# Sweeping groups of images: both halves' channel products first, then both halves' inverse y products

## What is computed

```python
def _fourier_layer(v, W1, W2):
    x_ft = jnp.fft.rfft2(v)
    out1 = jnp.einsum('bixy,ioxy->boxy', x_ft[:, :, :M1, :M2], W1)
    out2 = jnp.einsum('bixy,ioxy->boxy', x_ft[:, :, -M1:, :M2], W2)
    ...
    return jnp.fft.irfft2(out_ft, s=(Sx, Sy))
...
for i in range(L):
    x1 = _fourier_layer(v, W1, W2)
    x2 = jnp.einsum('bcxy,cd->bdxy', v, w_w[i]) + w_b[i][None, :, None, None]
    v = x1 + x2
    ... # normalised over images and pixels, then relu
```

## Time and profile before

| | |
|---|---|
| median of 3 runs | 2758.26 us (2756.05 to 2761.63) |
| profiled execution | 2755.14 us, its span 2753.4 us |
| TensorE busy | 2334.1 us, 85% of the span |
| VectorE busy | 1924.8 us, 70% |
| ScalarE busy | 1050.1 us, 38% |
| inverse y products, L794 | 24576 matmul records, 237 ns each on average |
| channel products, L1029 | 6144 matmul records in the three sweeps |
| mean DMA rate | 187 GB/s |

### The profile page before, as it was taken

How to read it: one execution, slowest core, us unless ns; L and a number is a source line. 1 busy time by engine, 2 the same in 40 slices (tenths; PEclk the granted TensorE clock), 3 DMA queues, 4 the chain that set the end, 5 groups by cost and what they waited for, 6 DMA issues and landing times. The chain is left out here.

```text
span 2753.4 us, 191399 instructions
## 1 busy us (share of the span) xinstructions
PE 2334.1 (85%) x88271; PEld 1444.0 (52%) x88271; DVE 1924.8 (70%) x3293; ACT 1050.1 (38%) x1799; POOL 500.5 (18%) x619
## 2 busy tenths in 40 slices
PE   5799999977999997789999975876499826899998
PEld 3466666644666665456666642222277712444444
DVE  5688888865888886668888854004588863677776
ACT  3433333352333332523333333002136623677776
POOL 1034422200444221024442200000223200000000
PEclk9899999997999999989999997898789958999999
DMA  3266666615999996179999964896234203788886
GB/s 86 57 152 168 170 163 163 170 40 186 322 322 320 313 314 185 58 253 325 328 315 310 311 215 159 314 415 118 81 93 113 66 14 82 125 141 143 144 141 100
DMA packets 243410, 515.84 MB, mean 187 GB/s; under 512 B 65423, under 2 KB 114895, under 8 KB 222223
## 3 DMA queue, kind: packets, MB, share of 16 engines
q1 hardware_dynamic: 233736, 504.07, 64.4%
q10 hardware_dynamic: 9495, 9.34, 1.6%
HBM read 295.39 MB, written 214.78 MB: 185 GB/s over the span
## 5 line engine op out<-in xcount | busy, mean ns | idle before, releaser
L923 ACT ACTIVATE p_v<-p_ps,k_scale_bias 128x1024 f32<-128x1024 f32 x384 | 441.8, 1200 | 883.8 <-PE p_ps L794 883.8
L904 POOL COPY k_xm<-p_sp 64x288 f32<-64x288 f32 x372 | 260.2, 700 | 1181.0 <-DVE p_sp L327 1164.8
L317 DVE STREAM_TRANSPOSE p_vt<-p_v 128x1024 f32<-128x1024 f32 x384 | 451.2, 1213 | 6.4 <-ACT p_v L923 6.4
L794 PEld LDWEIGHTS p_ps<-k_idfty,p_t 32*64 32x64 f32 x24576 | 292.0, 135 | 178.5 <-issue 178.4
L2201 DVE TENSOR_TENSOR x_ht<-x_ht,x_mask 128x384 f32<-128x384 f32 x512 | 262.0, 554 | 149.7 <-ACT x_ht L2172 102.2
L2172 ACT ACTIVATE x_ht<-x_ph,w_b 128x384 f32<-128x384 f32 x576 | 303.4, 578 | 142.4 <-PE x_ph L2224 142.4
L322 DVE STREAM_TRANSPOSE p_at<-p_ps 128x1024 f32<-128x1024 f32 x192 | 228.5, 1228 | 149.6 <-PE p_ps L295 149.6
L794 PE MATMUL p_ps<-k_idfty,p_t 32*64 32x64 f32 x24576 | 319.8, 237 | 10.7 <-issue 10.7
L803 PEld LDWEIGHTS p_ps<-p_vt 128*32 128x32 f32 x24576 | 219.6, 109 | 99.8 <-issue 99.8
L2224 PE MATMUL x_ph<-x_et,w_w 64*64 64x384 f32 x2304 | 247.0, 494 | 12.7 <-DMA x_et<-expert_inputs 6.4
L2240 PE MATMUL x_pe<-x_ht,w_w 64*64 64x384 f32 x2304 | 245.0, 489 | 11.3 <-DVE x_ht L2201 10.2
(11 more groups left out here) (329 smaller groups left out, 2625.4 us busy)
## 6 DMA issues: line engine op xcount, KB each, us to landing
field<-p_v SPq DMA_DIRECT2D x768, 256.0 KB, 5.8
p_v<-field SPq DMA_DIRECT2D x128, 1024.0 KB
x_mask<-expert_weights SPq DMA_DIRECT2D x32, 1536.0 KB, 14.8
l_v<-field SPq DMA_DIRECT2D x16, 2048.0 KB, 25.8
k_xm<-field SPq DMA_DIRECT2D x12, 2048.0 KB, 28.7
at_cf<-state_coefficients SPq DMA_DIRECT2D x32, 384.0 KB
k_mixw<-field SPq DMA_DIRECT2D x4, 2048.0 KB, 26.1
k_mixw<-in_L_tok_fw_dram SPq DMA_DIRECT2D x48, 144.0 KB, 4.4
```

Of the source, the lines that this page charges most:

```text
L317: return nc.vector.transpose(cols(vt), cols(px.rearrange("p (g m) -> p g m", g=G)))
L794: ins = nc.tensor.matmul(ps[64 * a1:64 * a1 + 64, g, col:col + S], lines, K["idfty"][rows, :], start=False, stop=True, skip_group_check=True)
L904: nc.gpsimd.tensor_copy(view[64 * k:64 * k + 64, :, j, :, G * i:G * i + G], sp[64 * j:64 * j + 64, :, :, 16 * k:16 * k + M1].rearrange("p ...
L923: nc.scalar.activation(field[:, 2 * q:2 * q + 2, CH * half:CH * half + CH], ps[:, e, 2 * q:2 * q + 2, :], ACT.Relu, bias=bias, scale=scale ...
```

## The change

In each group the channel products of both halves are issued first, and then the inverse y products of both halves. The wait of half 0 for its own inverse turn is dropped, since the wait of half 1 for both turns now stands ahead of both inverse y products. Prologue and loop are changed alike. The number of instructions other than that wait stays the same, and VectorE's, ScalarE's, GpSimd's and SP's orders aren't touched.

```diff
                         nc.tensor.matmul(ps[C * a:C * a + C, e, g, :], weights[rows, C * g:C * g + C], v[rows, 0, col:col + CH],
                                          start=True, stop=False, skip_group_check=True)
-                if half == 0:
-                    pe.wait_ge(s.t_ready, 2 * i + 1)
-                    pe.nop(nofuse=True)
-                inverse_y(nc, K, ps[:, e], st, half).then_inc(s.um_done, 1)
+
+            def rows(i):
+                for half in range(2):
+                    inverse_y(nc, K, ps[:, half], st, half).then_inc(s.um_done, 1)
...
             pixels(0, 0)
             pixels(0, 1)
+            rows(0)
             spectrum(1)
             with pe.Fori(1, n) as i:
                 pixels(i, 0)
                 pixels(i, 1)
+                rows(i)
                 forward(i - 1)
                 spectrum(i + 1)
```

## The result

The changed kernel takes 2948.5 us (median of 4 runs, 2941.6 to 2950.8) against 2758.0 before: a ratio of 1.068, with an interval from 1.067 to 1.070. The forecast was 2932 with a range from 2905 to 2985. So sign and size are right. The profiled execution took 2950.84 us, 195.7 more than that of before.

What follows compares the result with a forecast made beforehand. The prediction took a 13.42 us chain through VectorE and TensorE as the bound. Two waits lengthen it by 1.93 us a group, times 90 groups 174 us, giving 2932 us, range 2905 to 2985.

Steps and rivals of the forecast that it cites:

- What bounds before: Steady loop: a chain through VectorE, passing TensorE only in the y and x products, sets the 13.42 us period.
- First term, C1's wait: Channel products of half 1 wait for both inverse turns, now uncovered; this wait alone costs 0.92 us a group.
- Second term, the eviction: The next y product waits for ScalarE's eviction of half 0, now covered by one step only: 1.01 us late.
- Sum of the terms in the steady state: New period from y product to y product 15.35 us against 13.42, so 1.93 us more a group.
- Changes of shape: TensorE, two matmul shape changes fewer: saves nothing to 0.1 us; rival of at most 0.84 us a group, 2 in 100.
- DMA queues: Loads and stores don't set the pace; second sweep's DMA share loosens from 0.97 to near 0.85.
- The clock: TensorE's granted clock stays 1.00 despite new gaps; rival that it falls, 72 to 360 us more, 9 in 100.

Runs made afterwards that it cites:

- the old order: Kernel before, order unchanged, but the inverse y product of half 0 waits for both inverse turns; 2895.9 us, ratio 1.052.
- the kernel with that term gone: Changed kernel with all 32 rows in sweep one's channel products and, from third group on, both half 0 evictions cut to 32 of 512 columns; 2814.5 us.

## Why the prediction was right, point by point

- **What bounds before**: right. The wait put ahead of I0 lengthened the period, the work taken off VectorE's chain shortened it.
- **First term, C1's wait**, forecast 0.92: measured 0.73 with the old order. The hand-over was 0.11 and not the 0.15 taken, and I1 to Y was 1.57 and not 1.71, since the 1.71 held a wait for VectorE. Counting it as TensorE's own time was the slip, although the prediction itself puts TensorE's readiness 0.17 us ahead of Y.
- **Second term, the eviction**, forecast 1.01: 15.21 - 14.02 = 1.19 against the kernel with that term gone (1.06 in sweep one, 15.21 - 14.15). It is larger than forecast because TensorE's own path to Y was shorter (the same slip, and the order's 0.14). The whole chain was forecast at 15.35 and is 15.21: the eviction with its hand-over took 2.42 (842.91 to 845.33), not 2.52.
- **Sum of the terms in the steady state**: 1.93 forecast, 1.79 measured (0.73 - 0.14 + 1.19 = 1.78). In time, each kernel taken from its own before: first term 70 us, order -14, eviction 100, clock 35. These steps add up to the measured 191 by construction. The groups give the check: 70, -12, 103 and 42, together 203, less the 7 us at the starts of the sweeps and in the rest.
- **Changes of shape**: the prediction had "nothing to 0.1 us", on TensorE's side, which the new chain leaves idle. It is 0.14 us, and the second half is right: in the changed kernel Y is held by the eviction, so TensorE only idles longer by what the order saves, and the eviction's term is larger by the same 0.14. The Trainium skill's rule (TensorEngine Tiling (Array Packing), Key Properties: a change of tiling mode drains TensorE) has the right sign, at 0.14 us for the one change fewer on TensorE's path from the inverse turns to Y.
- **DMA queues**: right, share 0.85 in sweep two.
- **The clock**: the step that failed. "Short even gaps do little" held for sweeps two and three and not for one, which runs at 0.84 and costs 35 to 42 us. I had read sweep one as the same as sweep two because its period was the same. The form of its channel products, 4 rows for 32, was in the trace and I gave it no weight. That the total fitted is partly luck: the clock added 42 us by the groups, and the other errors, 0.14 us too much in each group (13 us) and 7 us at the starts, went the other way.

## What to carry to other kernels

A wait that costs nothing may be covered by a step between it and its cause; before moving such a step, write down which waits it covers on both sides, here the inverse turn ahead of it and the eviction behind it. Two engines that look full (97% and 86%) can still be bound by a chain through both, and then the place to gain is the engine's wait on that chain, however short. When a stage gets new pauses, look at how much of the array its matmuls use: where it is little, the clock may fall and add as much again or more (3.18 us a group instead of 1.79 here).

## What the runs showed of the hardware

- With pauses of 0.8 to 1.2 us in each 15 us, the granted clock stayed at 1.00 where channel products used 32 rows of a tile, and fell to 0.80 to 0.91 on average over stretches of 100 us (between its two levels, 1.2 and 2.4 GHz, within a group) where they used 4. Without the pauses 4 rows did no harm: sweep one before ran at 1.00. Rows of zeros restored it. How far it falls differs from run to run for the same code (16.60 and 16.02 us a group), and one pause of 0.86 us took it lower (0.81) than that pause and one ahead of Y together (0.84).
- Sixteen more matmuls in the loop took a pass of sweep one from 16.6 to 34.3 us, partly at half clock, with 3.96 MB more instructions loaded. Where between two and sixteen the border lies was not tried.
- One change of tile shape fewer (between 32 x 32 and 32 x 64) on TensorE's path saved 0.14 us a group where nothing else held the next step (14.16 to 14.02), though weight loads pause for 0.84 us at such a change.
